# A decoder kernel on one core: the normalising pass of three layer norms moved from VectorE to ScalarE, with a new order of steps

## The reference, cut to what matters

```python
x = _layernorm(x + attn(x))            # 16 heads of 8, softmax over keys, with a relative-position term on keys and on values
x = _layernorm(x + xattn(x, ctx))      # 16 heads of 8, causal softmax
x = _layernorm(x + ffn(x))             # one shared expert and 8 routed ones, the top 2 weighted; hidden width 256, gelu
def _layernorm(x, eps=1e-05):
    return (x - mean(x)) / sqrt(var(x) + eps)
```

## Time and profile before

| | |
|---|---|
| median of three runs | 485.68 us |
| the profiled execution's own time | 484.97 us |
| its span, first to last instruction | 482.9 us |
| mean granted TensorE clock | 0.929 of full speed |
| TensorE (PE) busy | 406.3 us |
| VectorE (DVE) busy | 324.4 us |
| ScalarE (ACT) busy | 248.0 us |
| GpSimd (POOL) busy | 76.4 us |

### The profile page before, as it was taken

The page is one execution under the profiler, slowest core; times in us unless marked ns, Lnnn a source line. Parts: engine busy times, 40 slices in busy tenths (PEclk is TensorE's granted clock), DMA queues, the critical chain, the costliest instruction groups (busy, mean ns, idle before and its releaser), DMA issues.

```text
span 482.9 us, 11287 instructions
## 1 busy us (share of the span) xinstructions
PE 406.3 (84%) x4718; PEld 302.9 (63%) x4729; DVE 324.4 (67%) x630; ACT 248.0 (51%) x329; POOL 76.4 (16%) x84
## 2 busy tenths in 40 slices
PE   3775399847879999999899899998999998649992
PEld 2464158734656877767688676776786767525772
DVE  4429953698868787887787868888975377143233
ACT  2470187703558583368774932487973425514340
POOL 9700000201340120003411100113101102410000
PEclk9776589959999999999999999999999999876998
DMA  4558025140013513001121630011110200000001
GB/s 107 156 113 261 3 68 155 35 121 5 3 36 88 175 47 99 3 18 44 37 68 23 166 99 1 4 36 24 49 24 1 81 20 3 2 23 0 2 0 23
DMA packets 29324, 26.87 MB, mean 56 GB/s; under 512 B 12577, under 2 KB 27866, under 8 KB 28506
## 3 DMA queue, kind: packets, MB, share of 16 engines
q1 hardware_dynamic: 28442, 26.02, 20.0%
q10 hardware_dynamic: 832, 0.13, 0.2%
HBM read 18.38 MB, written 7.35 MB: 53 GB/s over the span
## 4 chain that ended last, share of the span: by engine, by line
PE 55%; DVE 22%; ACT 8%; DMA 5%; issue 4%; SPq 4%; POOL 1%; POOLq 0%; DVEq 0%; ACTq 0%
PE ps_f L708 12%; PE ps_f L719 11%; PE ps_s L545 8%; PE ps_f L571 5%; PE ps_f L671 3%; DVE ST L930 3%; DVE ST L960 3%; DMA QS<-MP 3%; PE ps_f L579 2%; ACT ST L786 2%; DVE MX L933 2%; PE ps_s L538 2%; PE ps_f L518 2%; PE ps_f L524 2%; SPq L414 2%
## 5 line engine op out<-in xcount | busy, mean ns | idle before, releaser
L545 PE MATMUL ps_s<-QS,KS 125*128 125x128 bf16 (+1 forms) x768 | 80.6, 249 | 16.7 <-DVE ST L930 11.2
L545 PEld LDWEIGHTS ps_s<-QS,KS 125*128 125x128 bf16 (+1 forms) x768 | 64.4, 106 | 43.9 <-issue 14.9
L833 ACT ACTIVATE HT<-ps_f,hb 128x512 f32<-128x512 f32 x72 | 48.9, 689 | 81.5 <-PE ps_f L708 39.2
L719 PEld LDWEIGHTS ps_f<-w,HT 128*128 128x128 f32 x576 | 69.2, 192 | 10.0 <-issue 7.4
L708 PE MATMUL ps_f<-x2T,w 128*128 128x512 f32 x144 | 73.5, 619 | 0.0
L719 PE MATMUL ps_f<-w,HT 128*128 128x128 f32 x576 | 73.3, 278 | 0.0
L790 ACT ACTIVATE ST<-ST 128x1024 f32<-128x1024 f32 x32 | 33.6, 1060 | 52.1 <-DVE ST L960 51.7
L1044 DVE SCALAR_TENSOR_TENSOR acc<-ps_f,gw,acc 128x128 f32<-128x128 f32 x128 | 37.4, 363 | 31.3 <-PE ps_f L719 31.2
L483 POOL TENSOR_SCALAR_AFFINE_SELECT PC<-PC 128x1024 f32<-128x1024 f32 x32 | 34.8, 1096 | 147.8 <-ACT PC L797 147.7
L930 DVE TENSOR_TENSOR ST<-ps_s,ST 128x1024 f32<-128x1024 f32 x32 | 38.6, 1207 | 13.4 <-PE ps_s L545 13.4
L937 DVE TRANSPOSE_TENSOR_REDUCE MX<-ps_s 128x32 f32<-128x1024 f32 x32 | 39.0, 1237 | 7.1 <-PE ps_s L545 7.1
(11 more groups left out here) (114 smaller groups left out, 560.7 us busy)
## 6 DMA issues: line engine op xcount, KB each, us to landing
parts_by_head<-part SPq DMA_DIRECT2D x16, 384.0 KB, 2.7
QS<-parts_by_head SPq DMA_DIRECT2D x24, 256.0 KB, 3.8
KS<-parts_by_head SPq DMA_DIRECT2D x24, 256.0 KB, 4.9
xin<-in_x SPq DMA_DIRECT2D x16, 64.0 KB, 2.1
cin<-in_ctx SPq DMA_DIRECT2D x4, 256.0 KB, 4.5
w<-in_L_ffn_rw SPq DMA_DIRECT2D x1, 1024.0 KB
out_x<-acc SPq DMA_DIRECT2D x16, 64.0 KB, 1.8
QS<-MP SPq DMA_DIRECT2D x48, 8.0 KB, 2.1
```

The source lines that it names most:

```text
L545: last = nc.tensor.matmul(ps[:, o:o + S], KS[a][0:kd, c:c + S], queries(a, kd, h, j), start=not masked and j == 0, stop=j == NB - 1, skip_ ...
L719: last = nc.tensor.matmul(ps[:, b * E:(b + 1) * E], HT[n % 2][:, f, b * S:(b + 1) * S], w2[:, e, f, :], start=f == 0, stop=f == NF - 1 and ...
L833: nc.scalar.activation(HT[n % 2][:, f, :], ps[:, :], ACT.Gelu, bias=hb[:, e, f:f + 1]).then_inc(ht_ready, 1)
```

## The change

Three things are changed.

The last pass of each layer norm is made by ScalarE as `Identity(rstd * y + (-mean * rstd))`, four instructions of 128x128 with a scale and a bias taken from a column each. GpSimd makes the two columns: after the power it multiplies the mean by -1 (`negm`) and that by rstd (`nmr`).

Waits are added: statistics of a later chunk wait for GpSimd's last instruction of the chunk before; the division into `Y` (steps `X`, `cX`) waits until ScalarE has read `Y` for the layer norm before it; ScalarE waits where VectorE used to before it overwrites `x1` and `x2`.

The list is new. It holds the same 488 words in another order; the core of it is shown. A second constant tile (`minus`) raises a count that others wait for from 9 to 10, and the compiler's dynamic DMA scratch is set to 8192.

```diff
 SCHEDULE = """
-0load 1load 0xT 0q 0v 0k 0cT 0loadc 0st_q 0st_k 1xT 0ck 1q 0bias.0 0cv 0bias.1 0bias.2 0bias.3 0bias.4 0bias.5
-0bias.6 0bias.7 0p1.0 0p1.1 0p1.2 0p1.3 0p1.4 0p1.5 0m.0 0p1.6 0p1.7 0p2.0 0m.1 0p2.1 0p2.2 0p2.3 0pv.0 0p2.4
-0p2.5 0pv.1 0p2.6 0p2.7 0pvT.0 0pvT.1 0pv.2 1st_q 1k 0w2.0 0w2.1 0w2.2 0pv.3 0w2.3 0pvT.2 0pvT.3 0w2T.0 0w2T.1
-0w2T.2 0w2T.3 1bias.0 1loadc 1bias.1 0X 0XT 1bias.2 1bias.3 0o 1bias.4 1bias.5 1v 0ln 0st_ck 1st_k 1bias.6
-1bias.7 1p1.0 0x1T 0cq 1p1.1 1p1.2 0st_cq 1cT 1p1.3 1p1.4 2load 1m.0 0c1.0 0c1.1 0c1.2 0c1.3 1p2.0 1p2.1 0c1.4
...
-3c1.0 3c1.1 2up.14 3c1.2 3c1.3 2up.15 3c1.4 3cm.0 2up.16 3c1.5 3c1.6 2dn.6 2up.17 3c2.0 3c1.7 2dn.7 3c2.1 3cm.1
-3c2.2 3c2.3 3cpv.0 2dn.8 3c2.4 3c2.5 3cpv.1 3c2.6 3c2.7 3cpv.2 3cpvT.0 2fln 3cX 3cpvT.1 3cpv.3 3cpvT.2 3cpvT.3
-3cXT 3co 3cln 3x2T 3r 3up.0 3up.1 3up.2 3up.3 3g 3up.4 3dn.0 3up.5 3dn.1 3dn.2 3up.6 3up.7 3up.8 3up.9 3up.10
+0cT 0load 0loadc 0xT 0q 0v 0st_q 0k 0ck 0cv 0bias.0 0st_k 0bias.1 0bias.2 1load 0bias.3 0bias.4 0bias.5 0bias.6
+0bias.7 0p1.0 0p1.1 0p1.2 0p1.3 0p1.4 0m.0 0p1.5 1xT 0p1.6 0p1.7 0p2.0 0m.1 0p2.1 0p2.2 0p2.3 0pv.0 0p2.4 0p2.5
+0p2.6 0pvT.0 0p2.7 0st_ck 0pv.1 1q 1k 0w2.0 0w2.1 0pv.2 0w2.2 0w2.3 1st_q 0pvT.1 1st_k 0pv.3 1v 0pvT.2 0w2T.0
+0w2T.1 0pvT.3 0w2T.2 1bias.0 0w2T.3 1bias.1 1bias.2 0XT 1bias.3 0X 1bias.4 0o 1bias.5 1bias.6 1bias.7 1p1.0
+1p1.1 1loadc 0ln 0x1T 0cq 0st_cq 1p1.2 1p1.3 1p1.4 1m.0 0c1.0 0c1.1 0c1.2 2load 0c1.3 1p2.0 1p2.1 1p2.2 0c1.4
...
+1up.3 2cq 3p1.2 1up.4 1up.5 1dn.0 2st_cq 1dn.1 3p1.3 1up.6 1up.7 1up.8 1dn.2 1up.9 2c1.0 3cT 2c1.1 2c1.2 2c1.3
...
+3c1.4 3cm.0 3c1.5 2dn.6 3c1.6 2up.15 2up.16 2up.17 3c1.7 3c2.0 3cm.1 3c2.1 2dn.7 3c2.2 3c2.3 3cpv.0 3c2.4 3c2.5
+3cpv.1 3cpvT.0 3c2.6 3c2.7 3cpvT.1 3cpv.2 2dn.8 3cX 3cpv.3 3cpvT.2 3cpvT.3 3cXT 2fln 3cln 3co 3x2T 3r 3up.0
+3up.1 3up.2 3up.3 3g 3up.4 3up.5 3dn.0 3dn.1 3up.6 3up.7 3dn.2 3dn.3 3up.8 3up.9 3up.10 3up.11 3dn.4 3up.12
...
@@ gpsimd, at o, co and fln
                     g.wait_ge(ve_ready[k], ch + 1)
+                    if ch:
+                        g.wait_ge(ln_ready[k], ch)
                     nc.gpsimd.tensor_tensor(rstd[k][:, :], ve[k][:, :], halfm[:, :], ALU.pow).then_inc(rstd_ready[k], 1)
+                    nc.gpsimd.tensor_tensor(negm[k][:, :], mv[k][:, :, 0], minus[:, :], ALU.mult).then_inc(negmean[k], 1)
+                    g.wait_ge(rstd_ready[k], ch + 1)
+                    g.wait_ge(negmean[k], ch + 1)
+                    nc.gpsimd.tensor_tensor(nmr[k][:, :], negm[k][:, :], rstd[k][:, :], ALU.mult).then_inc(shift_ready[k], 1)
@@ scalar
+            def normalise(k, ch, y, o):
+                act.wait_ge(shift_ready[k], ch + 1)
+                for b in range(NB):
+                    last = nc.scalar.activation(o[:, b, :], y[:, b, :], ACT.Identity, bias=nmr[k][:, b:b + 1],
+                                                scale=rstd[k][:, b:b + 1])
+                last.then_inc(ln_ready[k], 1)
...
+                if what == "ln":
+                    if ch:
+                        act.wait_ge(y_ready[1], ch)
+                    normalise(0, ch, Y, x1)
+                elif what == "cln":
+                    if ch:
+                        act.wait_ge(dn_done, (NEXP + 1) * (ch - 1) + 1)
+                    normalise(1, ch, Y, x2)
+                elif what == "fln":
+                    normalise(2, ch, acc, acc)
@@ vector
             def statistics(k, ch, y):
+                if ch:
+                    v.wait_ge(shift_ready[k], ch)
...
-            def normalise(k, ch, y, o):
-                v.wait_ge(rstd_ready[k], ch + 1)
-                for b in range(NB):
-                    last = nc.vector.tensor_scalar(o[:, b, :], y[:, b, :], mv[k][:, b, 0:1], rstd[k][:, b:b + 1],
-                                                   ALU.subtract, ALU.mult)
-                last.then_inc(ln_ready[k], 1)
...
+                    before = [u for u in ORDER[:ORDER.index(s)] if u[1] in ("ln", "cln")]
+                    if before:
+                        v.wait_ge(ln_ready[int(before[-1][1] == "cln")], before[-1][0] + 1)
                     nc.vector.tensor_tensor(Y[:, :, :].rearrange("p b (h d) -> p b h d", h=H), X[a][:, :, :, 0:HD], den.broadcast_to([P, NB, H, HD]), ALU.mult).then_inc(X_ready[a], 1)
...
-    nc = bacc.Bacc("TRN2", target_bir_lowering=False, num_devices=1)
+    nc = bacc.Bacc("TRN2", target_bir_lowering=False, num_devices=1, dynamic_dma_scratch_size=8192)
```

More of the change, by code:

```diff
@@ new lines @@
+0w2T.1 0pvT.3 0w2T.2 1bias.0 0w2T.3 1bias.1 1bias.2 0XT 1bias.3 0X 1bias.4 0o 1bias.5 1bias.6 1bias.7 1p1.0
+1p1.1 1loadc 0ln 0x1T 0cq 0st_cq 1p1.2 1p1.3 1p1.4 1m.0 0c1.0 0c1.1 0c1.2 2load 0c1.3 1p2.0 1p2.1 1p2.2 0c1.4
+0cm.0 0c1.5 1pv.0 1pvT.0 1p2.3 0c1.6 0c1.7 0c2.0 0cm.1 0c2.1 1p1.5 1pv.1 1cT 2xT 0c2.2 1p1.6 0cpv.0 0c2.3 1p1.7
+0c2.4 1pvT.1 0cpvT.0 0cpv.1 1m.1 0c2.5 2q 0c2.6 0c2.7 0cpv.2 1p2.4 0cpvT.1 1p2.5 0cpv.3 1p2.6 1cv 0cpvT.2 1p2.7
+0cpvT.3 1pv.2 2v 2st_q 1pv.3 0cX 2k 1ck 1w2.0 0cXT 1w2.1 1w2.2 0co 2loadc 1pvT.2 1st_ck 2st_k 1w2.3 2bias.0
@@ new lines @@
+1pvT.3 1w2T.0 1w2T.1 3load 1w2T.2 0cln 2bias.1 1w2T.3 0x2T 1X 2bias.2 2bias.3 0r 1XT 2bias.4 0up.0 1o 0up.1
+2bias.5 2bias.6 0g 0up.2 2bias.7 2p1.0 0up.3 0dn.0 1ln 1x1T 2p1.1 0up.4 1cq 0dn.1 0up.5 0up.6 2p1.2 1st_cq 2cT
+2p1.3 0up.7 0up.8 0dn.2 0dn.3 0up.9 2m.0 0up.10 1c1.0 1c1.1 0dn.4 1c1.2 0up.11 1c1.3 0up.12 2p2.0 1cm.0 1c1.4
+0up.13 1c1.5 0dn.5 1c1.6 3xT 1c1.7 0up.14 2p1.4 0up.15 1c2.0 2p2.1 2p1.5 1c2.1 1cm.1 1c2.2 2p1.6 1cpv.0 1c2.3 3k
+1cpvT.0 2pv.0 2p1.7 1cpv.1 1c2.4 0dn.6 1c2.5 2pvT.0 1c2.6 2m.1 1cpvT.1 1c2.7 1cpv.2 2p2.2 2p2.3 1cpv.3 3loadc
@@ new lines @@
+2p2.4 2p2.5 1cpvT.2 2cv 2pv.1 1cpvT.3 2p2.6 2p2.7 0dn.7 2ck 2pv.2 2w2.0 3q 2w2.1 0up.16 2pvT.1 2w2.2 1cXT 3st_q
+1cX 2pvT.2 2pv.3 1co 2w2.3 3st_k 0up.17 2st_ck 2pvT.3 2w2T.0 2w2T.1 2w2T.2 3v 2w2T.3 1cln 2X 1x2T 3bias.0 1r 2XT
+3bias.1 0dn.8 3bias.2 3bias.3 1up.0 3bias.4 3bias.5 1up.1 0fln 2o 3bias.6 3bias.7 2ln 1g 3p1.0 3p1.1 1up.2 2x1T
+1up.3 2cq 3p1.2 1up.4 1up.5 1dn.0 2st_cq 1dn.1 3p1.3 1up.6 1up.7 1up.8 1dn.2 1up.9 2c1.0 3cT 2c1.1 2c1.2 2c1.3
+1up.10 2c1.4 2c1.5 1up.11 2cm.0 1dn.3 2c1.6 1up.12 2c1.7 1dn.4 1up.13 2cm.1 2c2.0 1dn.5 2c2.1 3m.0 2c2.2 3p1.4
@@ new lines @@
+2c2.3 2cpv.0 2c2.4 3p1.5 2cpvT.0 2cpv.1 2c2.5 3p2.0 1dn.6 2c2.6 3p1.6 2cpv.2 2c2.7 1up.14 3p1.7 2cpvT.1 1up.15
+2cpv.3 2cpvT.2 3m.1 2cX 1up.16 2cpvT.3 1up.17 3p2.1 3p2.2 1dn.7 2cXT 3p2.3 3p2.4 3cv 1dn.8 3pv.0 3pv.1 3p2.5
+3pvT.0 3p2.6 3p2.7 3pvT.1 2co 3ck 3pv.2 3w2.0 2cln 3w2.1 3w2.2 2x2T 1fln 3pv.3 2r 3w2.3 3pvT.2 3pvT.3 3w2T.0
+3w2T.1 3w2T.2 2up.0 3w2T.3 3X 3st_ck 2up.1 2g 3XT 2up.2 3o 2up.3 2dn.0 3ln 2up.4 2dn.1 3x1T 2up.5 3cq 2up.6
+2up.7 3st_cq 2up.8 2dn.2 2up.9 2dn.3 2up.10 2up.11 2dn.4 2dn.5 3c1.0 3c1.1 2up.12 3c1.2 2up.13 3c1.3 2up.14
@@ L187, in build @@
         rstd = [sb(f"rstd{i}", [P, NB]) for i in range(3)]
+        nmr = [sb(f"nmr{i}", [P, NB]) for i in range(3)]
+        negm = [sb(f"negm{i}", [P, NB]) for i in range(3)]
+        minus = sb("minus", [P, NB])
         x1 = sb("x1", [P, NB, E])
@@ L258, in build @@
         rstd_ready = [sem(f"rstd_ready{i}") for i in range(3)]
+        negmean = [sem(f"negmean{i}") for i in range(3)]
+        shift_ready = [sem(f"shift_ready{i}") for i in range(3)]
         ln_ready = [sem(f"ln_ready{i}") for i in range(3)]
@@ L456, in _ @@
             nc.gpsimd.memset(maskT[:, :, :], 0.0).then_inc(c_pool, 1)
-            g.wait_ge(c_pool, 6)
+            nc.gpsimd.memset(minus[:, :], -1.0).then_inc(c_pool, 1)
+            g.wait_ge(c_pool, 7)
             nc.gpsimd.affine_select(out=maskT[:, :, :], in_=maskT[:, :, :], compare_op=ALU.is_ge, fill=MASKED,
@@ L464, in _ @@
             nc.gpsimd.tensor_copy(identb[:, :], ident[:, :]).then_inc(c_pool, 1)
-            g.wait_ge(c_pool, 9)
+            g.wait_ge(c_pool, 10)
             zeros(1)
@@ L750, in _ @@
                     weights(1)
-                if what in ("xT", "x1T", "x2T", "cT", "XT", "cXT"):
+                if what == "ln":
[8 more added lines that the diff above has]
+                    normalise(2, ch, acc, acc)
+                elif what in ("xT", "x1T", "x2T", "cT", "XT", "cXT"):
                     dst = x2T if what == "x2T" else transposed(s)
@@ L983, in _ @@
                     statistics(a, ch, Y)
-                elif what == "ln":
-                    normalise(0, ch, Y, x1)
-                elif what == "cln":
-                    normalise(1, ch, Y, x2)
                 elif what == "r":
@@ L1049, in _ @@
                     statistics(2, ch, acc)
-                    normalise(2, ch, acc, acc)
 _ATTN = ["Wq", "bq", "Wk", "bk", "Wv", "bv", "Wo", "bo"]
```

24 lines of the change are left out of this document (3 added, 21 removed).

## The result

The kernel after takes **511.23 us** (median, 510.26 to 511.66) where the kernel before took 485.03 on the same chip: ratio 1.0554, 95% interval 1.0493 to 1.0615. The profiled execution took 511.09 us with a span of 509.0. The forecast was 489.2 with a range to 494.0: slower as said, but by 26 us instead of 4.

A forecast was written before the change was run, and what follows sets the result against it. TensorE was taken as the bound in the middle, chains of short steps and DMAs at both ends. Terms summed to +3.55 us on 484.97, 488.5; with 0.7 for the median of runs, 489.2 us, range 481.0 to 494.0.

The forecast's parts named there:

- Start: Start of the kernel: with the new order, the first score pass on VectorE begins later, +1.5 us (0.6 to 3.5).
- `1xT`: Chunk 1's x lands behind the experts' data, so TensorE waits and VectorE's score passes stop: +2.6 us (0 to 4.5).
- Before `0X`: Stretch ahead of `0X`: `1q` and `1v` now lie there, 2.2 us of TensorE work, costing +1.4 us (0 to 2.2).
- +0.7: Behind `0X`: less to do in idle time, and `1cT` still to be done when `0c1.0` starts, +0.7 us.
- Three norms on the path: `0ln`, `3cln` and the last `fln` lie on the path, each 0.95 us longer: 2.85 us in all.
- The saturated stretch: Middle, 143.6 to 396.6 us, TensorE nearly always busy: few of its 8.3 idle us belong to VectorE, -1.5 us (-4 to +3).
- The other nine have expert matmuls or a neighbour chunk's scores beside them: The nine remaining norms are covered by other work and add nothing; without cover, 0.95 us each.
- ScalarE's waits in place: Rival: ScalarE stands still at norms, delaying copies and gelus; nine at 0.5 us, 495.2 us in all, chance 0.10.
- `X` waits for ScalarE: At `X` and `cX` VectorE waits until ScalarE has read `Y`: 0, up to 1 us each if the pair closes up.
- Table loads: On ScalarE: switches between exponential and gelu fall from 16 to 14, 2.6 us off a non-bounding engine, 0 in the sum.
- Chunk 3: Tail of the kernel: new order puts `3cm.1` earlier, so `3cX` comes near 420.9 instead of 424.87: -4.0 us (-5 to -1).

The follow-up runs named there:

- e7: Kernel after with `1load` as third step, and `1xT` and `1q` just ahead of `0bias.0`: 506.66 us, ratio 1.0487 to the kernel before.
- e16: Kernel before (pass on VectorE), old list up to step 77 and new list from step 78, `3co` ahead of `3cln`: 496.28 us, ratio 1.0237.
- e2: Kernel before (pass on VectorE) with the new list, only `3co` put ahead of `3cln`: 515.51 us, ratio 1.0607.
- e3: Kernel after (pass on ScalarE) with steps 0 to 77 in the old order, the rest new: 500.87 us, ratio 1.0322 to the kernel before.
- e1: Kernel after with the old list, only `2cln` put ahead of `2x2T`: 511.7 us, ratio 1.0569 to the kernel before.
- e17: Kernel before, with ScalarE waiting for rstd and making four dummy Identity instructions at `2ln` alone: 486.85 us, ratio 1.0073.
- e12: Kernel after with the old list and a tile Y of its own for each attention: 513.28 us, ratio 1.0616 to the kernel before.
- e13: Kernel before (pass on VectorE), old list up to step 392 and new list from step 393, `3co` ahead of `3cln`: 484.31 us, ratio 0.9993.
- e19: As e17, with TensorE repeating matmuls of `3bias.6` (made twice) and `3bias.7` (four times) in its gaps: 485.67 us, ratio 1.0020 to the kernel before.

## Why the prediction was wrong, point by point

- **Start, +1.5, and `1xT`, +2.6: right.** Measured 1.5 and 2.4, with the mechanisms named, the last x at 53.55 included.
- **"Before `0X`", +1.4 (0 to 2.2): mis-sized, 5.8.** The step costed TensorE's matmuls of `1q` and `1v`. The writes, the stackings and the queue of SyncE behind `1q` and `1k`, and `1bias.0` in front of `0w2T.3`, were not counted. An earlier `1q` gives 3.3 of the 5.8 back (`e7`); the rest is not placed. Up to `0c1.0` the start costs 11.0 us; the terms up to there summed to 7.15. The last two of them, +0.7 and 0.95, became 1.35 together.
- **Three norms on the path, 3 x 0.95: right.** From the sum in Y to `0x1T` it takes 5.64 us against 4.76, from `3cX` to the first expert matmul 13.1 against 12.1, from the last statistics to the end 8.4 against 7.35.
- **"The saturated stretch", -1.5 (-4 to +3): the step that failed.** Its own check was that TensorE's idle time there must not change by more than 4 us. It changed by 12.8, and the stretch by 14.3. The term weighed VectorE's relief against ScalarE's waits in place and put the new order of these steps at nothing, though start and chunk 3 were each given a price for theirs. The runs show the order in its place: with the pass on VectorE the stretch from `0cX` to `3X` is 16 us (`e16`) and 15 us (`e2`) longer than before, with the pass on ScalarE 14 (`e3` and the kernel after). Some 5 of the 12 us of added idle time are TensorE's waits for norms that now stand close ahead of their readers; what makes the rest stays open.
- **"The other nine have expert matmuls or a neighbour chunk's scores beside them": wrong in the old order.** There the pass on ScalarE costs 27 us (`e1`). ScalarE was taken for the least loaded engine and its 1.6 us for work in free time, but at a norm its queue holds copies that TensorE needs within a microsecond or two: the cover was taken away by what it should have covered. In the list that the kernel after has, this cost doesn't come out of the noise.
- **The rival "ScalarE's waits in place"** had the mechanism of the old order, at nine times 0.5 us. One norm measured alone costs 3.4 us in all (`e17`), and at `2ln` the trace has 3.6. The price left out the work behind the wait and the clock behind the gap. For the kernel after it names the wrong cause as well: no rival priced the order of the middle. That it had the direction right is luck.
- **`X` waits for ScalarE, 0: right** (`e12`). **Table loads, 0**: nothing in the traces speaks against it. **Chunk 3, -4.0: 1.7 in the trace, 0 by itself** (`e13`).

TensorE's clock was read in the earlier trace rows as 1.00 for the middle and taken as given. It held while TensorE had hardly a gap there (8.3 us idle of 253). The Trainium skill ("TensorE: Matmul & The Clock Gate", "HAM oscillation — how this bites in real kernels") describes the same: a wait between bursts sets the array back, and the next burst starts at the lower rate. The windows of `e17` and `e19` agree, 0.53 against 1.00 behind the same step.
